# The norm stage of a graph, mixer and expert kernel: edge lists first, x tile by tile, scaling on ScalarE

## The reference, cut to what matters

```python
x1 = x + mix(layernorm(x)) + gnn(layernorm(x), edges)   # 1250 rows of 768
out = x1 + experts(layernorm(x1))                        # top-2 groups, top-2 experts
def layernorm(x): return (x - mean(x)) / sqrt(var(x) + 1e-5)
# mix: qkv = xn @ qkv_w.T + b, then linear attention with random features, 8 heads of 96
# gnn: two attention layers over 41250 edges (src, dst), sorted by dst, 1250 self loops among them
```

## Time and profile before

| | us |
|---|---|
| median of three runs | 2323.49 |
| the profiled execution, its own time | 2322.11 |
| its span in the profile | 2320.4 |
| PE busy in the span | 2104.9 (91%) |
| DVE busy | 1120.2 (48%) |
| first instruction of the norm block to the first of the mixer block | 0 to 67.36 |
| first projection matmul (L700) of half 0 | 80.70 |

### The profile page before, as it was taken

One profiled execution on the slowest core, in us unless ns is written; L12 is line 12 of the kernel. 1 busy time (PEld: TensorE's weight loads), 2 busy tenths in 40 slices (PEclk: granted clock), 3 DMA queues, 4 the chain that ended last, 5 costly groups with the idle time before them and its releaser, 6 DMA issues. The chain is left out here.

```text
span 2320.4 us, 32855 instructions
## 1 busy us (share of the span) xinstructions
PE 2104.9 (91%) x9786; PEld 1454.7 (63%) x9787; DVE 1120.2 (48%) x2406; ACT 400.1 (17%) x733; POOL 188.4 (8%) x182
## 2 busy tenths in 40 slices
PE   1799989998799999699999889989985899999997
PEld 0466666665463444488888755545572677777776
DVE  4456646556273530488888600226536333433333
ACT  0121221112101321122222200001010122222221
POOL 0000000000000000000000000000001233333322
PEclk9899999999899999899999999999965899999999
DMA  5200031001625530333333264431035588898754
GB/s 145 96 18 15 17 128 52 15 17 53 171 84 166 163 108 1 121 112 108 118 101 96 64 235 135 163 117 54 22 117 197 150 252 254 244 290 255 200 139 75
DMA packets 80595, 282.26 MB, mean 122 GB/s; under 512 B 11036, under 2 KB 31488, under 8 KB 70913
## 3 DMA queue, kind: packets, MB, share of 16 engines
q1 hardware_dynamic: 56207, 210.50, 27.1%
q0 software_dynamic: 14048, 51.06, 9.5%
q10 hardware_dynamic: 10258, 19.61, 2.7%
HBM read 222.26 MB, written 58.87 MB: 121 GB/s over the span
## 5 line engine op out<-in xcount | busy, mean ns | idle before, releaser
L1157 PE MATMUL gat_Z<-h,gat_wt 125*125 125x256 f32 (+1 forms) x1600 | 354.6, 381 | 18.0 <-DVE gat_wt L1073 18.0
L1157 PEld LDWEIGHTS gat_Z<-h,gat_wt 125*125 125x125 f32 x1600 | 298.0, 188 | 63.6 <-DVE gat_wt L1073 18.8
L700 PE MATMUL mix_G<-mix_w,xnT 128*125 128x384 f32 x720 | 245.6, 492 | 10.3 <-POOL mix_count_zero L602 10.3
L1975 PE MATMUL ex_PH<-ex_xT,ex_w 128*128 128x128 f32 x1872 | 224.8, 280 | 1.8 <-issue 0.5
L1305 PE MATMUL gat2p_Y<-gat2p_w,gat2p_hT 128*125 128x386 f32 (+1 forms) x640 | 209.6, 489 | 10.3 <-DMA gat2p_w<-in_L_gnn_W 10.3
L1975 PEld LDWEIGHTS ex_PH<-ex_xT,ex_w 128*128 128x128 f32 x1872 | 215.8, 194 | 2.8 <-issue 2.8
L1985 PE MATMUL ex_PY<-ex_w,ex_hT 128*128 128x384 f32 x624 | 214.8, 494 | 2.2 <-ACT ex_hT L1924 2.0
L941 PE MATMUL first_G<-gnn_w,xnT 128*125 128x512 f32 x480 | 208.3, 593 | 0.0
L700 PEld LDWEIGHTS mix_G<-mix_w,xnT 128*125 128x125 f32 x720 | 134.0, 190 | 97.2 <-issue 15.6
L1305 PEld LDWEIGHTS gat2p_Y<-gat2p_w,gat2p_hT 128*125 128x125 f32 x640 | 120.1, 188 | 98.4 <-issue 12.4
L1985 PEld LDWEIGHTS ex_PY<-ex_w,ex_hT 128*128 128x128 f32 x624 | 114.3, 190 | 78.7 <-ACT ex_hT L1924 4.7
(11 more groups left out here) (291 smaller groups left out, 2207.6 us busy)
## 6 DMA issues: line engine op xcount, KB each, us to landing
ex_w<-in_L_ffn_W SPq DMA_DIRECT2D x64, 1152.0 KB, 9.1
gat_cnt<-c_dram SPq DMA_DIRECT2D x50, 546.9 KB
gat2p_hT<-h1T_dram SPq DMA_DIRECT2D x20, 1000.0 KB, 5.0
h1T_dram<-gat_oT ACTq DMA_DIRECT2D x40, 250.0 KB
ct_dram<-mix_count_out SPq DMA_DIRECT2D x40, 157.0 KB, 2.0
mix_w_slice<-in_L_gnn_W SPq DMA_DIRECT2D x6, 1024.0 KB, 11.9
proj_w2s<-in_L_gnn_W SPq DMA_DIRECT2D x4, 1536.0 KB, 26.4
gnn_w<-in_L_gnn_W SPq DMA_DIRECT2D x4, 1536.0 KB, 10.6
```

The source lines that it names most:

```text
L700: last = pe.matmul(G[c][:], xnT[:, k, t * P:(t + 1) * P], w[:, k, c, :], start=(k == 0), stop=(k == KD - 1))
L1157: last = pe.matmul(Z[b][j][:], wt[b][:, s, :], h[:, s, bass.ds(hd, 1), j * HC:(j + 1) * HC + j], start=(s == 0), stop=(s == NT - 1))
L1975: last = pe.matmul(PH[m][:], w1[:, b, k, m * 128:(m + 1) * 128], xT[:, k, :], start=(k == 0), stop=(k == KD - 1))
```

## The change

Everything is in the norm block, but for the four counting constants.

- Edge lists. Partition p now holds three consecutive rows of 128 edges, so one list is three loads (96 partitions, 11 partitions, the last 162 edges). SP loads dst, ACT loads src, ahead of x. The copies at the end (L258 before) reorder the columns back.
- x comes tile by tile, even tiles on SP, odd ones on ACT, each with a semaphore of its own. The random features and the mixer's weights follow on SP.
- DVE's list is reordered: edges, then statistics in three groups (tiles 0 to 2, 3 to 6, 7 to 9), each with its own variance, root and refinement, and only after the first four copies the window search, with further copies between its steps.
- The scaling moves from DVE to ACT: Identity with scale rstd and bias -mean*rstd, into a ring of three buffers instead of two.
- POOL makes the counting constants in the norm block, ahead of partition_all_reduce, once for both halves. c_consts and its waits are gone.

```diff
-            sp.wait_ge(blank, 2)
-            for v, t in ((dst, di), (src, si)):
-                for g in range(2):
-                    sp.dma_start(t[:, g, :], v[g * EGP * ER:(g + 1) * EGP * ER].rearrange("(p e) -> p e", e=ER)
-                                 ).then_inc(loaded, 16)
...
+        def load_edges(eng, t, v):
+            for lo, hi_ in ((0, 96), (96, FULL)):
+                eng.dma_start(t[lo:hi_, :, :].rearrange("p g e -> p (g e)"),
+                              v[lo * PE_ROWS:hi_ * PE_ROWS].rearrange("(p e) -> p e", e=PE_ROWS)).then_inc(loaded, 16)
+            eng.dma_start(t[FULL:FULL + 1, :, :].rearrange("p g e -> p (g e)")[:, 0:REST],
+                          v[FULL * PE_ROWS:EDGES].unsqueeze(0)).then_inc(loaded, 16)
...
             sp.wait_ge(blank, 2)
+            load_edges(sp, di, dst)
+            for t in range(0, NT, 2):
+                rows_dma(sp, xa[:, t, :], x[t * P:(t + 1) * P, :], x_loaded[t])
+            sp.dma_start(rfT[0:MD, :], rf_dram).then_inc(rf_loaded, 16)
+            load_next(sp)
...
+            pool.iota(ikey[:], [[1, 128]], base=0, channel_multiplier=0, **kw)
+            pool.iota(islo[:], [[1, SLO]], base=0, channel_multiplier=0, **kw)
+            pool.iota(off[:], [[WIN * SPLIT, NW]], base=0, channel_multiplier=0, **kw)
+            pool.memset(czero[:], 0.0)
             pool.wait_ge(span_ready, 1)
             pool.partition_all_reduce(allb[:], best[:], EGP, bass.bass_isa.ReduceOp.max).then_inc(span_max, 1)
...
+            def scale(g):
+                lo, hi_ = GROUPS[g]
+                dve.wait_ge(sqrt_done, g + 1)
+                refine_rstd(step, dve, rstd[:, lo:hi_], std[:, lo:hi_], veps[:, lo:hi_], tmp[:, lo:hi_])
+                dve.scalar_tensor_tensor(shift[:, lo:hi_], mv[:, lo:hi_, 0], -1.0, rstd[:, lo:hi_], ALU.mult, ALU.mult
+                                         ).then_inc(scale_ready, 1)
...
+            stats_of(*GROUPS[0])
+            variance(0)
+            stats_of(*GROUPS[1])
+            scale(0)
+            variance(1)
+            stats_of(*GROUPS[2])
+            scale(1)
+            variance(2)
+            copy(0)
+            scale(2)
+            for t in range(1, 4):
+                copy(t)
+
             dve.wait_ge(iotas, 2)
...
+                copy(4 + g)
+            copy(7)
+            for j, dest in enumerate((keyT, sloT)):
+                dve.wait_ge(turned, j + 1)
+                dve.tensor_copy(dest[:].rearrange("k (p g) -> k g p", g=EG),
+                                T[j][:].rearrange("k (g p) -> k g p", g=EG)).then_inc(copied, 1)
+            copy(8)
             dve.wait_ge(span_max, 1)
...
+            copy(9)
...
+            act.wait_ge(blank, 2)
+            load_edges(act, si, src)
+            for t in range(1, NT, 2):
+                rows_dma(act, xa[:, t, :], x[t * P:(t + 1) * P, :], x_loaded[t])
...
+            root(0)
+            for t in range(3):
+                normalise(t)
+            root(1)
+            copy(0)
+            root(2)
+            for t in range(3, NT):
+                normalise(t)
+                copy(t - 2)
+            copy(NT - 2)
+            copy(NT - 1)
...
-                pool.iota(ikey[:], [[1, 128]], base=0, channel_multiplier=0, **kw).then_inc(c_consts, 1)
-                pool.iota(islo[:], [[1, SLO]], base=0, channel_multiplier=0, **kw).then_inc(c_consts, 1)
-                pool.iota(off[:], [[WIN * SPLIT, NW]], base=0, channel_multiplier=0, **kw).then_inc(c_consts, 1)
-                pool.memset(czero[:], 0.0).then_inc(c_consts, 1)
...
-                pe.wait_ge(c_consts, 4)
```

More of the change, by code:

```diff
@@ L131, in norm_phase @@
     dve_step = cx.sem("norm_dve_step")
[L132 to L135, removed]
+    ikey, islo, off, czero = counting
+    PE_ROWS = EG * ER
+    FULL = EDGES // PE_ROWS
+    REST = EDGES - FULL * PE_ROWS
+    assert FULL < EGP and EGP * EG == EROWS
     with ExitStack() as st:
@@ L143, in norm_phase @@
         rstd = sb(nc, st, "rstd", [P, NT])
-        xn = [sb(nc, st, f"xn{b}", [P, D]) for b in range(2)]
+        shift = sb(nc, st, "shift", [P, NT])
+        xn = [sb(nc, st, f"xn{b}", [P, D]) for b in range(RING)]
         di = sb(nc, st, "edge_di", [EGP, EG, ER], I32)
@@ L255, in _, with root, normalise, copy @@
                                    ALU.logical_shift_right))
-            for j, dest in enumerate((keyT, sloT)):
-                dve.wait_ge(turned, j + 1)
-                dve.tensor_copy(dest[:], T[j][:]).then_inc(copied, 1)
+            copy(9)
         @block.scalar
         def _(act):
[L262 to L269, removed]
+            act.wait_ge(blank, 2)
+            load_edges(act, si, src)
+            for t in range(1, NT, 2):
+                rows_dma(act, xa[:, t, :], x[t * P:(t + 1) * P, :], x_loaded[t])
+            def root(g):
+                lo, hi_ = GROUPS[g]
+                act.wait_ge(veps_done, g + 1)
+                act.activation(std[:, lo:hi_], veps[:, lo:hi_], ACT.Sqrt).then_inc(sqrt_done, 1)
+            def normalise(t):
+                g = [lo <= t < hi_ for lo, hi_ in GROUPS].index(True)
+                act.wait_ge(scale_ready, g + 1)
+                if t >= RING:
+                    act.wait_ge(transposed, t - RING + 1)
+                act.activation(xn[t % RING][:], xa[:, t, :], ACT.Identity, scale=rstd[:, t:t + 1],
+                               bias=shift[:, t:t + 1]).then_inc(xn_ready, 1)
+            def copy(t):
                 act.wait_ge(transposed, t + 1)
                 act.activation(xnT[:, 3:6, t * P:(t + 1) * P], tp[t % 2][1][:], ACT.Copy).then_inc(used_act, 1)
+            root(0)
[9 more added lines that the diff above has]
+            copy(NT - 1)
         @block.tensor
@@ L286, in _ @@
                 for k in range(KD):
-                    last = pe.transpose(tp[t % 2][k // 3][:, k % 3, :], xn[t % 2][:, k * 128:(k + 1) * 128],
+                    last = pe.transpose(tp[t % 2][k // 3][:, k % 3, :], xn[t % RING][:, k * 128:(k + 1) * 128],
                                         ident[0:P, 0:P])
@@ L2064, in build @@
                                    attn, ins["L0_gnn_W1"], ins["L0_gnn_att_src1"], ins["L0_gnn_att_dst1"], wa, keyT,
-                                   sloT, spans, ct_dram, load_half(1) if half == 0 else load_proj)
+                                   sloT, spans, counting, ct_dram, load_half(1) if half == 0 else load_proj)
                 proj_phase(nc, cx, attn, w_proj, proj_loaded, ins["L0_mix_proj_b"], ins["L0_gnn_b2"], x, x1_dram,
```

58 lines of the change are left out of this document (35 added, 23 removed).

## The result

The kernel after takes 2281.99 us (median of 4 runs, 2279.98 to 2287.72); the kernel before took 2323.51 beside it on the same chip (2319.66 to 2324.63). The ratio is 0.9828, interval 0.9807 to 0.9849. That is 41.5 us less. 2289 was forecast, 34.4 less. The profiled execution took 2279.98 around a span of 2278.2, against 2320.4 before: 42.2 less.

The account below looks back on a forecast made before the run. PE is busy for 91% of the span, but in the first two slices every engine waits. Block 26.5 + constants 10.3 + clock 0 - switch 2.4 = 34.4 us less, giving 2289 us; range 2283 to 2298.

Parts of the forecast that it names:

- the block: Norm block: its end was to move from 67.07 to 40.6 us, 26.5 us earlier.
- Edges: Norm block: edge loads issued first land at 5.5 us, at latest 10; DVE is free for x at 10.2.
- x: Norm block: x by tiles, last pair there at 22 us; DVE keeps up and is through scale(2) at 28.6.
- ACT: Norm block: a scaling costs ACT 1.02 us; its copies end at about 39.3, 1.3 us short of being the bound.
- Order of the list: Norm block: DVE's reordered work, costed only within the path to the block's end at 40.6 us.
- Counting constants: Mixer half 0: PE's wait of 10.3 us for the constants goes; half 1 gains nothing.
- The clock: First 36 projections: 2.2 us lost to the low clock; booked 0 back, up to 2.2 possible.
- The switch comes back: Route block's first iota: POOL's code switch of 11.8 us moves there, costing PE 2.4 us, between 0 and 11.8.
- Rival A: Route block: the switch costs nothing later; gain 36.8 us, time 2284.5 to 2287; chance 0.17.
- B: Mixer start: PE's 10.3 us wait stays, held by something else; gain 24.1 us, time 2299; chance 0.07.
- C: Norm block: small loads are slow, x there at 35 us; time 2302, or 2296 for half; chance 0.12.
- D: Mixer start: slower than before if weights on SP land after about 77 us; about 2331 at 85; chance 0.02.

Follow-up runs that it names:

- e6: Kernel after with the edge lists in their old shapes, still ahead of x on two queues; 2291.43 us.
- e9: Kernel after with the window search put ahead of x's statistics, as in the kernel before; 2286.87 us.
- e4: Kernel after with the scaling back on DVE, ACT only copying; 2289.46 us.
- e3: Kernel before with only the new loads (edges reshaped, first, on two queues; x tile by tile); 2296.09 us.
- e1: Kernel before with only the four counting constants moved to the norm block ahead of the reduction, c_consts gone; 2313.95 us.
- e2: Kernel after with the counting constants made in each mixer half again and waited for; 2291.65 us.
- e5: Kernel after with one small unread iota added in the mixer's half 0, behind a wait for the fifth tile's queries; 2282.82 us.
- e10: Kernel after with one small unread iota directly behind the partition_all_reduce in the norm block; 2286.58 us.
- e11: The kernel of e9 with one small unread iota directly behind the partition_all_reduce; 2281.13 us.
- e7: Kernel after with x loaded in two halves as before, one on each queue behind the edge list; 2293.46 us.

## Why the prediction was right, and where its sizes were off

The mechanism held in every step, and 34.4 of 41.5 us were forecast. The time came out at the lower edge of the range of 2283 to 2298: the ratio 0.9828, which takes in all runs, makes 2283.5 of 2323.49, just inside, and the median 2281.99 is 1.0 below. By spans the difference is 42.2 - 34.4 = 7.8 us, and it falls into four terms: the block 2.6, the wait for the constants 0.4, the clock behind it 1.5, and a drift in the later stages of 3.4 (1.4 up to the route block, 2.0 in the expert block). The sum of these is 7.9.

**Edges.** Predicted there at 5.5, measured 5.3. DVE was to be free for x at 10.2 and was at 9.95. That the landing came out is in part luck: it was taken from one store of 157 KB, and the prediction said nothing of the shape. In their old shape, just as early on the same two queues, the edges are there at 10.9 (e6).

**x.** The last pair was to be there at 22, by the slow end of the rate. It can't have been much off: tile 8 was taken at about 21.2 and tile 9 at 22.28. The term that was mis-sized is what DVE still owes then. Two tiles from 22.5 on made 24.4; DVE was through at 23.3, since it had tile 8 before its pair was complete. The 1.9 us for scale(2) with its wait for the root were 1.15, because copy(0) hid the root. scale(2) ended at 26.36 and not at 28.6: 2.2 of the 2.6 us. The tail behind it took 11.6 against 12.0.

**ACT.** 1.01 to 1.03 us for a scaling, predicted 1.02. The two rows behind the 88 ns for a pointer operand differ also in function and output type, so the agreement doesn't show the price of an operand. ACT was to be 1.3 us short of being the bound; its last copy ends at 36.45 and DVE's at 38.00. e9 runs into it, e4 shows DVE's list as the bound.

**Order of the list.** Costed as part of one path, and never by itself. e3 and e4 show that I would have credited the wrong edit: the loads give 25.9, the order and ACT's scaling together 3.15, and the order without ACT's scaling a loss.

**Counting constants.** 10.3 us predicted. e1 measured 10.4 to the first projection, e2 10.65 of wait. Between the end of the block and the first projection the shift grows by 10.67 (39.74 - 29.07); 10.33 of it is the wait, 0.12 the clearing of the banks (2.27 us for 2.39), and 0.2 that the first projection now begins before the modelled end of the clearing.

**The clock.** Booked at 0 with a bound of 2.2; it gave 1.5 (14.30 to 12.81) and 1.9 in e1. I argued that PE idles 3 us at the barrier anyway. True, but what it had lost lay in the 10.3 us behind that: in the kernel after, the stretch from 40 to 45 us has a granted clock of 0.70 and the next one 1.00, where before it was at 0.50 up to 85 us and the first projections ran there.

**The switch comes back.** 2.4 us predicted; the shift falls from 42.6 to 40.2. PE was to be held until 1761.1 less the shift, and is until 1761.04 (1718.44 + 42.60). The gap was 11.08 us for 11.8, and POOL's instructions from the iota to rt_cum took 0.5 longer than before (6.57 for 6.09): two small errors that happen to cancel. e1 (2.0) shows the cost alone, e5 takes it away (2.3). Rival A is refuted: the copies and memsets of the blocks in between don't bring the code back. The Trainium skill, GPSIMD Engine Reference, section Instruction dispatch, has some 6 us for such a load. e10 agrees, with 6.69 us on idle DMA engines. But in nine kernels it took 10.2 to 12.1 us beside engines that moved some 400 GB/s, so for a switch beside weight loads the row was the right price (7.34 beside x in e11): by the page's figure the slack of 9.3 would have hidden it.

**The rivals.** B (PE's wait stays) falls by e1. C (small loads are slow) falls by e3 and e7: the small pieces were faster for this block, not slower. D needed a weight after 77 us; they landed by 35, by the stretch that drops to 121 GB/s.

**The drift** of 3.4 us is in stages that the change doesn't touch, and its cause stays open. Comparing DVE's instructions one by one, the shift is 41.2 at 100 us of the kernel before, 41.8 at 200, 42.4 at 580, 43.7 at 627, 42.8 at 1000 and 42.6 at the route block; behind that it wanders from 40.2 to 42.2 through the expert block. The stage in front of the route block, which was 13 us shorter in e6, has no part in it here: POOL waits 42.90 us through it before and 42.99 after, both times at a clock of 0.50. The mixer at 250 us, which e9 shows at two levels, is not it either, since the shift is 41.8 in front of the place and 41.7 behind it. The forecast had no term for such a drift. Here it lay on the side of the gain, and with the other three terms, which lie on that side too, it brought the time to the edge of the range.

## What to carry to other kernels

Where two loads are needed in sequence by one engine, issue the first-needed one first, on both queues, in few loads with long rows (e6), and cut the second to the consumer's tile: that was 26 of 29 us here, against 3 for a new order of the consumer's list with the scaling on another engine. A switch of GpSimd's code is not removed by moving an iota, only handed to the next iota; send a small iota ahead in a place where POOL has nothing else to do, before the loads of the next block fill the DMA engines; what it gave here, 2.3 us, is seen in the profiles only. After the loads are right, ACT ended 1.6 us before DVE, so the next edit to either list is worth little: of the variants tried here, the best, e5 and e11, can't be told from the kernel after by their times.

## What the hardware showed unexpectedly

- The change of POOL's code between partition_all_reduce and an iota took 6.69 us with no transfer under way, 7.34 beside the loads of x at 248 GB/s, and 10.2 to 12.1 in nine kernels beside weights at 356 to 431 GB/s. The pair of instructions that brings it isn't held back by the semaphore wait of the iota behind it (e5: pair at 39.1, iota at 136.6). A pair alone doesn't mean such a gap: in front of the first iota of each kernel stands a pair too (at 1.8 us), with 0.30 us of idle time.
- One TENSOR_TENSOR of 125 x 40 on DVE took 1.93 us in e5 (the row at 1703.40), beside POOL's copies, and the same operation 0.20 us in the kernel after, where POOL stood in its gap. So with POOL standing still DVE has rt_sele ready 1.9 us sooner, of which PE has nothing, since it then waits for POOL. The row in the kernel after:

```profile
1703.15 0.20 DVE L1710 TENSOR_TENSOR rt_gate<-rt_gate,rt_mx 125x40 f32<-125x40 f32 x1
```

- The stage in front of the route block runs at either level of the clock, 43.7 us long at 0.50 and 30.5 at 0.94 to 1.00, in kernels that are the same there. The mixer at 253 us differs in the same way by 2.2 us (e9).
